# Attention megakernel on one core: row sums of squares of keys and queries taken without single-column products

## The reference, cut to what matters

```
q = silu(conv(x W_q)); k = silu(conv(x W_k)); v = silu(conv(x W_v))
q = q * rsqrt(mean(q*q) + 1e-6) * 128**-0.5 * 128**-0.5
k = k * rsqrt(mean(k*k) + 1e-6) * 128**-0.5
M = strictly_lower((beta * k) @ k.T * decay)
T = inverse(I + M)
v_c = T @ (beta * v);  k_cumdecay = T @ (beta * k * exp(g))
for each chunk: attn = (q @ k.T) * decay; v_new = v_c - k_cumdecay @ state; ...
h = core * rsqrt(mean(core*core) + 1e-6);  out = (norm_w * h * silu(z)) @ W_out.T
```

## Time and profile before

| | us |
|---|---|
| median of 3 runs | 3787.94 |
| lowest, highest | 3785.24, 3791.33 |
| the profiled execution | 3785.71 |
| its span, first to last instruction | 3783.8 |
| mean granted TensorE clock | 0.982 |
| TensorE busy | 3344.6 (88%) |
| VectorE busy | 2453.1 (65%) |
| ScalarE busy | 1968.5 (52%) |
| GpSimd busy | 1505.5 (40%) |

### The profile page before, as it was taken

The page is one execution under the profiler, slowest core; times in us unless marked ns, Lnnn a source line. Parts: engine busy times, 40 slices in busy tenths (PEclk is TensorE's granted clock), DMA queues, the critical chain, the costliest instruction groups (busy, mean ns, idle before and its releaser), DMA issues. The chain is left out here.

```text
span 3783.8 us, 58251 instructions
## 1 busy us (share of the span) xinstructions
PE 3344.6 (88%) x18978; PEld 2619.3 (69%) x18978; DVE 2453.1 (65%) x5143; ACT 1968.5 (52%) x4746; POOL 1505.5 (40%) x2617
## 2 busy tenths in 40 slices
PE   0114999999999999999999999999999999999987
PEld 0113777777777777777777777777777777777763
DVE  6873566666666666666676666666666666666643
ACT  5762555554555555555555555555555555555531
POOL 9963343433433343434344333434333433334310
PEclk9998999999999999999999999999999999999988
DMA  2013222222222222222222222222222122222202
GB/s 95 33 50 135 70 73 73 72 54 71 75 74 64 67 62 76 75 75 69 53 70 77 72 68 72 54 76 76 73 75 70 51 78 70 74 66 66 56 5 100
DMA packets 291213, 261.53 MB, mean 69 GB/s; under 512 B 220992, under 2 KB 249792, under 8 KB 281152
## 3 DMA queue, kind: packets, MB, share of 16 engines
q1 hardware_dynamic: 281696, 123.60, 13.5%
q10 hardware_dynamic: 9216, 134.22, 9.6%
HBM read 228.11 MB, written 29.62 MB: 68 GB/s over the span
## 5 line engine op out<-in xcount | busy, mean ns | idle before, releaser
L638 PE MATMUL x<-xs,w_high 128*128 128x512 f32 x3072 | 1063.4, 427 | 40.0 <-POOL w_low L1229 34.6
L638 PE MATMUL x<-xs,w_low 128*128 128x512 f32 x1536 | 613.6, 399 | 0.0
L873 ACT ACTIVATE uvec<-rb,cpos 128x128 f32<-128x128 f32 x512 | 160.1, 364 | 868.5 <-PE rb L658 868.5
L638 PEld LDWEIGHTS x<-xs,w_high 128*128 128x128 f32 x3072 | 531.3, 193 | 104.5 <-POOL w_low L1229 35.5
L937 ACT ACTIVATE slot<-lane 128x512 fp32r<-128x512 f32 x640 | 350.8, 608 | 402.1 <-PE lane L764 401.7
L1212 POOL TENSOR_TENSOR block_step<-block_in 64x14 f32<-64x14 f32 (+6 forms) x896 | 229.1, 256 | 506.3 <-DMA block_in<-blocks_dram 385.6
L1244 POOL TENSOR_TENSOR rstd<-rarg,powers 128x8 f32<-128x8 f32 x64 | 105.4, 1647 | 625.8 <-DVE rarg L1046 625.8
L638 PEld LDWEIGHTS x<-xs,w_low 128*128 128x128 f32 x1536 | 292.4, 190 | 67.8
L764 PEld LDWEIGHTS lane<-pinv,slot 128*128 128x128 f32 x1536 | 200.2, 192 | 190.2 <-ACT slot L937 98.9
L1009 DVE SCALAR_TENSOR_TENSOR cacc<-x,cwqk,cacc 128x511 f32<-128x511 f32 (+2 forms) x384 | 281.2, 746 | 44.3 <-ACT cacc L860 22.4
L1009 DVE SCALAR_TENSOR_TENSOR cacc<-x,cwv,cacc 128x511 f32<-128x511 f32 (+2 forms) x384 | 281.7, 747 | 37.9 <-ACT cacc L860 4.1
(11 more groups left out here) (203 smaller groups left out, 7737.2 us busy)
## 6 DMA issues: line engine op xcount, KB each, us to landing
xs<-mix_dram ACTq DMA_DIRECT2D x64, 2048.0 KB, 7.7
gb<-cum_dram SPq DMA_DIRECT2D x128, 256.0 KB, 4.4
w_in<-in_w_qkvz SPq DMA_DIRECT2D x48, 512.0 KB, 4.1
w_out<-in_w_out SPq DMA_DIRECT2D x16, 512.0 KB, 4.7
blocks_dram<-bt SPq DMA_DIRECT2D x512, 8.0 KB, 1.5
inverse_dram<-block_out SPq DMA_DIRECT2D x64, 128.0 KB, 2.2
inv<-inverse_dram SPq DMA_DIRECT2D x512, 16.0 KB, 1.8
side_kv<-in_side SPq DMA_DIRECT2D x4, 1024.0 KB, 11.5
```

The lines of the kernel that those rows point to most:

```text
L638: ins = mm(PROJ_BANK[kind][i][:, :], w, x, start=(k == 0 and j == 0), stop=(k == KC - 1 and j == 2))
L873: ins = a(uvec[:, h, :], rb[:, sl(h, HD)], ACT.Copy, scale=sm2[p]["cpos"][:, ch, h:h + 1])
```

## The change

TensorE: instead of 8 single-column products it runs 4 transposes of the queries (`query_tokens`), which put the tokens into the partitions, in the same place and into the same bank `x1`. ScalarE: `squares_qk` goes; instead it squares the transposed queries (128x512, out of `x1`) one slot later, behind the copies of product 1 and ahead of those of product 2. VectorE: the sums of squares of the keys are the diagonals of the key-key products that are made anyway; at slot 10 it multiplies bank `x0` with the identity and reduces along the row (`key_sums`); at slot 12, ahead of `small`, it reduces the squared queries (`query_sums`). `small` reads the sums from the new tile `sums`.

```diff
+        sums = sb("sums", [P, 2, NCH])
...
-            def key_sums(l, m):
-
-                W("sq_ready", l + 1)
+            def query_tokens(l, m, p):
+
                 if m is not None:
                     W("z_ready", 2 * m + 1)
-                for i in range(2):
-                    for ch in range(NCH):
-                        ins = mm(x1[:, 4 * i + ch:4 * i + ch + 1], sq[:, i, sl(ch, CH)], t["ones"][:, :], start=True, stop=True)
-                ins.then_inc(S["sums_full"], 1)
+                for ch in range(NCH):
+                    ins = nc.tensor.transpose(x1[:, sl(ch, HD)], qkT2[p][:, 1, sl(ch, CH)], ident[:, :])
+                ins.then_inc(S["qtok_full"], 1)
...
                     elif k == 10:
                         if L:
-                            key_sums(l, m)
+                            query_tokens(l, m, p)
...
-            def squares_qk(p):
-                act.drain()
-                a(sq[:, :, :].rearrange("p i s -> p (i s)"), qkT2[p][:, :, :].rearrange("p i s -> p (i s)"), ACT.Square).then_inc(S["sq_ready"], 1)
+            def query_squares(l):
+                W("qtok_full", l + 1)
+                a(sq[:, 0, :], x1[:, :], ACT.Square).then_inc(S["squares_ready"], 1)
...
-                        elif k == 9:
-                            squares_qk(p)
+                        elif k == 10:
+                            query_squares(l)
...
+            def key_sums(l):
+
+                work = sq[:, 1, :].rearrange("p (c s) -> p c s", s=CH)
+                W("kk_full", l + 1)
+                v.tensor_tensor(work, x0[:, :].rearrange("p (c s) -> p c s", s=CH), ident[:, :].unsqueeze(1).to_broadcast([P, NCH, CH]), ALU.mult)
+                dve.drain()
+                v.tensor_reduce(sums[:, 0, :], work, AX.X, ALU.add)
+
+            def query_sums(l):
+
+                W("squares_ready", l + 1)
+                v.tensor_reduce(sums[:, 1, :], sq[:, 0, :].rearrange("p (c s) -> p c s", s=CH), AX.X, ALU.add)
+
             def small(m, p):
 
                 dve.drain()
-                W("sums_full", m + 1)
                 W("masked", 2 * m + 2)
-                v.tensor_scalar(skt[:, :], x1[:, 0:4], HD * EPS, None, ALU.add)
-                v.tensor_scalar(qe[p][:, :], x1[:, 4:8], HD * EPS, HD * EPS * HD * EPS, ALU.mult, ALU.add)
+                v.tensor_scalar(skt[:, :], sums[:, 0, :], HD * EPS, None, ALU.add)
+                v.tensor_scalar(qe[p][:, :], sums[:, 1, :], HD * EPS, HD * EPS * HD * EPS, ALU.mult, ALU.add)
...
+                        elif k == 10:
+                            key_sums(l)
                         elif k == 12:
+                            query_sums(l)
                             small(l, p)
```

More of the change, by code:

```diff
@@ L511, in attention_phase @@
                  "v_tap0_ready qk_tap0_ready v_conv_done qk_conv_done v_ready qk_ready z_ready "
-                 "zeros_ready gathered block_in_loaded block_inverted block_stored inv16_loaded sq_ready sums_full sk_ready exps_ready irk_ready ktok_full ktok_ready kk_full kq_products_full vtok_full "
+                 "zeros_ready gathered block_in_loaded block_inverted block_stored inv16_loaded qtok_full squares_ready sk_ready exps_ready irk_ready ktok_full ktok_ready kk_full kq_products_full vtok_full "
                  "vtok_ready gneg_ready masked decay_ready b_ready lower_ready "
```

## The result

| | before | changed |
|---|---|---|
| median, us (4 runs each) | 3789.49 | 3686.41 |
| lowest, highest | 3785.24, 3791.33 | 3679.66, 3687.86 |
| profiled execution | 3785.71 | 3679.66 |
| its span | 3783.8 | 3677.9 |
| mean granted clock | 0.982 | 0.988 |

The ratio is 0.9726, 95% interval 0.9709 to 0.9743: 103 us less between the medians, 101 were predicted.

What follows compares the result with a forecast made beforehand. The prediction took TensorE's own work as the bound in the attention stage: 3785.7 us less 85 for its records and 16 for clock falls gives 3684.7, stated as 3685, range 3675 to 3706.

Steps and rivals of the forecast that it cites:

- The sum: Whole kernel: 85 us of TensorE records and 16 us of clock falls off the profiled 3785.7 us.
- TensorE as the bound: Attention stage: TensorE's work plus 1.3 us of waits makes the 51.5 us iteration; 1.33 us saved in each, 85 us.
- The falls of the clock: Attention stage, z projection behind slot 10: eleven short falls to 1.2 GHz, 1.49 us each, expected to go, 16 us.
- Rival B: Attention stage: eleven or so clock falls stay, behind 12 transposes in a row; 3701 us, 12%.
- ScalarE at no cost: Slots around the copies of products 1 and 2: the new square, 0.6 us, ends 0.1 us ahead of need; cost 0.
- Rival C: Product 2 or the head transposes: TensorE newly waits for ScalarE, half of the 1.33 us lost; 3727 us, 9%.
- VectorE at no cost: Key and query sums: three added instructions fit VectorE's idle time, 1.45 us left ahead of product 4's sums; cost 0.

Runs made afterwards that it cites:

- ScalarE's move alone: Changed kernel with ScalarE's decays of head 1 moved behind its copies of product 5, VectorE's order kept: 3697.52 us.
- both moves together: Changed kernel with TensorE's key-token wait moved to key-query products, ScalarE's head 1 decays behind product 5's copies, VectorE's head 1 key matrix behind product 6's sums: 3559.53 us.

## Why the prediction was right

The sum was 85 + 16 = 101 us. The profiles show 1.30 us an iteration (1.75 - 0.45) where 1.33 was taken, 83 us; and eleven falls of 1.49 us gone, 16 us. That is 99. The medians lie 103 apart and the two profiled spans 106; 7 us of the latter are the last round, which no term of the sum names and which runs at either clock whatever the kernel. Some of the medians' 103 is likely that too, so part of the close agreement is luck.

- **TensorE as the bound** held: waits as before, iteration 51.5 to 50.2 us. That the price is one of records and not of columns was an inference from like spacings; 64 columns at the same time show it.
- **The falls of the clock** went, and the wide products and the sixteen transposes tell why: behind 16 single-column records there were eleven falls, behind 16 records with 64 columns or 16 transposes in the same place none. Rival B (12%) leaned on the rule about transposes. Two things bound this reading. With 8 single-column records there was no fall either. And single-column products are not the only cause: one fall came with five more reductions and two with ScalarE's move alone, each behind a wait of 1.5 to 1.6 us and without any such product. The prediction's clock of 1.0 "but for 11 short falls" also leaves out the first iteration: from 395 to 420 us the clock is 0.84 before and 0.91 in the changed kernel.
- **ScalarE at no cost** held, with 0.39 us to spare where I had worked out 0.1, and with more behind it than I had counted on. Rival C did not come.
- **VectorE at no cost** held. A reduction of 512 took 0.68 us, 0.1 more than a quarter of the long one and far from its upper bound; the slack was 1.72 where I had left 1.45, for the reduction begins right behind the gated heads and the gap of 0.15 us ahead of the sums that I had added was in the old order already. Where this slack is used up, the prediction had each us paid ahead of product 5. The five reductions show it paid ahead of product 7, because product 6 waits for ScalarE anyway.
- **What the prediction missed** lies beside the sum: it took TensorE's waits as printed, 1.3 us an iteration. It needed only that they stay, which they did. As an estimate of what is left to gain they were short by a third: both moves together took 125 us, 1.95 an iteration.

## What to carry to other kernels

Where TensorE is the bound, as here, records with 1, 64 and 128 moving columns cost the same 0.11 us (one of 512 columns took 0.23), so sums over partitions by a ones column are paid at the price of products with 128 columns. Where a product that is made anyway holds the sums, reading them on an engine with slack is worth its two extra passes. Look at what the clock does behind such narrow products, and behind a wait that a change makes longer. Read a wait from start to start of the products around it, and move the copy that TensorE waits for and the engine that would be late next in one step, since one of them alone can lose, as ScalarE's did.

## What was not expected of the hardware

- 24 transposes in a row (2.6 us) left the clock at 2.4 GHz in all 31 windows from 420 to 3520 us, while 16 single-column records and 8 transposes in the same time brought it to 1.2 GHz eleven times.
- The clock fell also without narrow products, three times in two kernels, each time behind a wait of 1.52 or 1.57 us, while one of 1.58 us brought none; waits of 0.73 us in every iteration of the changed kernel brought no fall.
- A wait printed as 0.73 us was 1.29 us of start-to-start time.
- VectorE's reduction of 128x512 out of a tile takes 0.68 us, as long as a masked read of the same size from a bank (0.69).
